# Routed experts of an adaLN transformer block: gate and up products with the weights as the stationary operand

## The reference

```
h = layernorm(x) * (1 + ca) + sa
x = x + ga * attention(h)            # 16 heads of 16, LoRA on q, k, v and o
h = layernorm(x) * (1 + cb) + sb
x = x + gb * ffn(h)

def ffn(x):                          # x: (4096, 256)
    shared = swiglu(x, shared_gate, shared_up, shared_down)      # hidden size 512
    logits = x @ gate_w.T                                        # 8 experts
    top_id, score = argmax(logits), sigmoid(max(logits))
    xs = x * score
    for e in range(8):
        xe = where(top_id == e, xs, 0)
        routed += swiglu(xe, r_gate[e], r_up[e], r_down[e])
    return shared + routed

swiglu(x, wg, wu, wd) = (silu(x @ wg.T) * (x @ wu.T)) @ wd.T
```

## Time and profile before

| | |
|---|---|
| time, median of 3 runs | 1984.91 us (1983.95 to 1985.33) |
| the profiled execution | 1989.11 us, of it 1987.3 us from first to last instruction |
| PE busy | 1877.3 us (94%) |
| DVE busy | 1559.1 us (78%) |
| ACT busy | 1183.3 us (60%) |
| POOL busy | 342.1 us (17%) |
| mean granted clock of PE | 0.974 of full speed |
| routed stage, 1745.8 us to the end | 241.5 us |

### The profile page before, as it was taken

How to read it: one execution, slowest core, us unless ns; L and a number is a source line. 1 busy time by engine, 2 the same in 40 slices (tenths; PEclk the granted TensorE clock), 3 DMA queues, 4 the chain that set the end, 5 groups by cost and what they waited for, 6 DMA issues and landing times.

```text
span 1987.3 us, 33453 instructions
## 1 busy us (share of the span) xinstructions
PE 1877.3 (94%) x12334; PEld 703.0 (35%) x12335; DVE 1559.1 (78%) x2738; ACT 1183.3 (60%) x1386; POOL 342.1 (17%) x425
## 2 busy tenths in 40 slices
PE   7687999999999999999999999999976799999997
PEld 5332222222222222222222222222225555666664
DVE  5276999999999999999999999999717532244453
ACT  4533777777777777777777777777851221111111
POOL 5534200000000000000000000000025532223332
PEclk9897999999999999999999999999997799999999
DMA  4541111111111111211111111111056333222221
GB/s 157 167 148 37 41 41 39 61 57 42 41 54 60 44 41 44 66 50 38 41 60 57 44 38 54 56 43 38 12 179 227 119 114 110 94 83 67 69 66 48
DMA packets 89735, 141.50 MB, mean 71 GB/s; under 512 B 13104, under 2 KB 60208, under 8 KB 89472
## 3 DMA queue, kind: packets, MB, share of 16 engines
q1 hardware_dynamic: 74336, 102.01, 16.2%
q0 software_dynamic: 10240, 32.40, 5.0%
q10 hardware_dynamic: 5024, 5.24, 0.8%
HBM read 90.84 MB, written 48.51 MB: 70 GB/s over the span
## 4 chain that ended last, share of the span: by engine, by line
PE 81%; DVE 9%; DMA 3%; POOL 2%; issue 2%; ACT 1%; SPq 1%; POOLq 0%; DVEq 0%; ACTq 0%
PE ps L881 24%; PE ps L870 19%; PE ps L847 15%; PE ps L1561 7%; DVE mx L937 6%; PE ps L1111 5%; PE ps L1579 3%; PE ps L1445 3%; DMA l_in<-inverse_sums 2%; PE ps L587 1%; ACT prob L962 1%; POOL parts L727 1%; PE ps L1570 1%; POOL rest L723 1%; PE ps L915 1%
## 5 line engine op out<-in xcount | busy, mean ns | idle before, releaser
L937 DVE TENSOR_REDUCE mx<-ps 128x1 f32<-128x512 f32 x2048 | 1273.9, 684 | 59.1 <-PE ps L847 56.2
L962 ACT ACTIVATE prob<-ps 128x1024 f32<-128x1024 f32 x1024 | 992.4, 1021 | 274.8 <-PE ps L870 272.3
L881 PE MATMUL ps<-prob,vs 128*32 128x512 f32 x4096 | 546.4, 605 | 0.7 <-ACT prob L962 0.7
L847 PE MATMUL ps<-k_high,q_high 64*128 64x512 bf16 x2048 | 401.1, 388 | 33.8 <-DMA k_low<-qk_parts 17.3
L870 PE MATMUL ps<-q_high,k_high 64*128 64x512 bf16 x2048 | 390.1, 378 | 2.9 <-ACT prob L962 1.8
L870 PE MATMUL ps<-q_low,k_low 34*128 34x512 bf16 x2048 | 390.3, 378 | 0.0
L847 PEld LDWEIGHTS ps<-k_high,q_high 64*128 64x128 bf16 x2048 | 99.2, 93 | 669.7 <-DVE mx L937 628.7
L1016 POOL CAST mb<-turned_sb 16x128 bf16<-16x128 f32 x32 | 8.9, 280 | 926.2 <-ACT turned_sb L975 897.2
L870 PEld LDWEIGHTS ps<-q_low,k_low 34*128 34x128 bf16 x2048 | 100.1, 94 | 117.3 <-issue 0.7
L1610 ACT ACTIVATE esig<-ps 128x512 f32<-128x512 f32 x39 | 23.3, 597 | 195.9 <-PE ps L1561 195.9
L870 PEld LDWEIGHTS ps<-q_high,k_high 64*128 64x128 bf16 x2048 | 101.5, 96 | 88.5 <-ACT prob L962 29.6
(11 more groups left out here) (146 smaller groups left out, 1357.7 us busy)
## 6 DMA issues: line engine op xcount, KB each, us to landing
k_high<-qk_parts SPq DMA_DIRECT2D x128, 128.0 KB
qk_parts<-parts SPq DMA_DIRECT2D x32, 384.0 KB, 3.5
q_high<-qk_parts SPq DMA_DIRECT2D x128, 64.0 KB
k_low<-qk_parts SPq DMA_DIRECT2D x128, 64.0 KB
head_out<-head_out_sb SPq DMA_DIRECT2D x32, 256.0 KB, 10.8
sorted_in<-zero_row POOLq DMA_DIRECT2D x13, 390.0 KB, 7.3
xs<-sorted_in SPq DMA_DIRECT2D x39, 130.0 KB
q_low<-qk_parts SPq DMA_DIRECT2D x128, 32.0 KB
```

The costliest lines, as they stand in the source:

```text
L847: pe.matmul(ps[:, ring.bank((n, m, u)), :], q_high[p][mine, t * P:(t + 1) * P], k_high[p][mine, c * CH:(c + 1) * CH], start=True, stop=Tru ...
L881: mm = pe.matmul(ps[32 * j:32 * j + 32, 7, :], vs[buf(h)][:, kt, :], prob[:, kt % 2, j * CH:(j + 1) * CH], start=(kt == 0), stop=(kt == KT ...
L937: dve.tensor_reduce(mx[n % 2][:, at, c:c + 1], ps[:, ring.bank(what), :], AX.X, ALU.max).then_inc(s_ring, 1)
L962: act.activation(prob[:, kt % 2, :].rearrange("p (u c n) -> p u c n", u=2, c=2)[:, :, half, :], ps[:, 2 * half:2 * half + 2, :], ACT.Exp). ...
```

## The change

`rgT` and `ruT` stay as they are, but PE no longer reads them. For every tile ACT copies the chosen expert's gate weights to a fixed buffer `gate_w` and its up weights to `up_w` (two buffers of each, 128 x 1024 fp32). ACT reads the expert of the tile into a register for that, three turns ahead of the tile. In `gate_or_up` the operands change places: 128 columns of the weights are stationary, and the tile's 128 tokens are streamed. The product comes out with hidden units on the partitions, so DVE writes `ehT` directly from silu and up product; the four transposes, their PSUM bank, `ehid`, and ACT's copy out of PSUM are gone. PE waits for `gate_w` and `up_w`. `gate` and `up` now follow each other, and `down` stays last in the turn. Some buffers change their place in SBUF: `eout` and `cix` move out of the region of `h2T`, and `gate_w` and `up_w` lie in it.

```
-            def gate_or_up(k, e, w, bank, done):
+            def gate_or_up(k, w, bank, done):
                 u = pair(k)
-                if isinstance(k[0], int) and tnum(k) == 1 and w is rgT:
+                for fc in range(FC):
+                    for c in range(HALF):
+                        mm = pe.matmul(ps[:, bank, fc * P:(fc + 1) * P], w[u][:, c, fc * P:(fc + 1) * P],
+                                       xsT[u][:, c, :], start=(c == 0), stop=(c == 1))
+                mm.then_inc(done, 1)
+
+            def gate(k):
+                if isinstance(k[0], int) and tnum(k) == 1:
                     pe.wait_ge(s_x2, NCH + 1)
-                for c in range(HALF):
-                    mm = pe.matmul(ps[:, bank, :], xsT[u][:, c, :], w[:, bass.ds(e, 1), c, :].squeeze(1),
-                                   start=(c == 0), stop=(c == 1))
-                mm.then_inc(done, 1)
-
-            def turn_hidden(k):
-                u = pair(k)
-                pe.wait_ge(s_ehid, tnum(k) + 1)
-                wait(pe, s_ehT, tnum(k))
-                for c in range(FC):
-                    mm = pe.transpose(ps[:, 5, c * P:(c + 1) * P], ehid[u][:, c * P:(c + 1) * P], ident[:])
-                mm.then_inc(s_ehTp, 1)
+                pe.wait_ge(s_xsT, tnum(k) + 1)
+                pe.wait_ge(s_gate_w, tnum(k) + 1)
+                wait(pe, s_esig, tnum(k) - 1)
+                gate_or_up(k, gate_w, egate_bank(k), s_egate)
+
+            def up(k):
+                pe.wait_ge(s_up_w, tnum(k) + 1)
+                wait(pe, s_ehT, tnum(k) - 1)
+                gate_or_up(k, up_w, eup_bank(k), s_eup)
...
                 if next1:
-                    e = expert_of(next1)
-                    pe.wait_ge(s_xsT, tnum(next1) + 1)
-                    wait(pe, s_esig, tnum(next1) - 1)
-                    gate_or_up(next1, e, rgT, egate_bank(next1), s_egate)
-                if this:
-                    turn_hidden(this)
-                if next1:
-                    wait(pe, s_ehid, tnum(next1) - 1)
-                    gate_or_up(next1, e, ruT, eup_bank(next1), s_eup)
+                    gate(next1)
+                    up(next1)
                 if next2:
                     turn_in(next2)
                 if this:
                     down(this)
...
-            def take(k):
+            def weights(k):
+
                 u = pair(k)
-                act.wait_ge(s_ehTp, tnum(k) + 1)
-                wait(act, s_ey, tnum(k) - 1)
-                act.copy(ehT[u][:].rearrange("p c n -> p (c n)"), ps[:, 5, :]).then_inc(s_ehT, 1)
+                e = act.value_load(tile_e[0:1, bass.ds(tnum(k), 1)], min_val=0, max_val=E - 1)
+                wait(act, s_egate, tnum(k) - 1)
+                act.copy(gate_w[u][:], rgT[:, bass.ds(e, 1)].squeeze(1)).then_inc(s_gate_w, 1)
+                wait(act, s_eup, tnum(k) - 1)
+                act.copy(up_w[u][:], ruT[:, bass.ds(e, 1)].squeeze(1)).then_inc(s_up_w, 1)
 
             def turn(k):
                 if later(k, 1):
                     silu(later(k, 1))
-                if later(k, 0):
-                    take(k)
-
-            turns(act, turn, 1)
+                if later(k, 3):
+                    weights(later(k, 3))
+
+            act.wait_ge(s_route, 1)
+            act.wait_ge(s_expert, 48 * E)
+            turns(act, turn, 3)
...
-                wait(dve, s_ehTp, tnum(k) - 1)
-                dve.tensor_tensor(ehid[u][:], esig[u][:], ps[:, eup_bank(k), :], ALU.mult).then_inc(s_ehid, 1)
+                wait(dve, s_ey, tnum(k) - 1)
+                dve.tensor_tensor(ehT[u][:].rearrange("p c n -> p (c n)"), esig[u][:].rearrange("p c n -> p (c n)"),
+                                  ps[:, eup_bank(k), :], ALU.mult).then_inc(s_ehT, 1)
```

More of the change, by code:

```diff
@@ L285, in block_kernel @@
         xs = buffers("xs", [P, XW], F32, r, NX)
-        r = Region(nc, stage_at, experts_at)
+        cix = buffers("cix", [P, 1], U32, r, NX)
+        eout = buffers("eout", [P, D], F32, Region(nc, after_h2T, after_h2T + 2 * 4 * CH), NX)
+        r = Region(nc, stage_at, after_h2T)
         xsT = buffers("xsT", [P, HALF, P], F32, r)
-        esig = buffers("esig", [P, F], F32, r)
-        ehid = buffers("ehid", [P, F], F32, r)
+        esig = buffers("esig", [P, FC, P], F32, r)
         ehT = buffers("ehT", [P, FC, P], F32, r)
-        eout = buffers("eout", [P, D], F32, r, NX)
         x2_in = buffers("x2_in", [P, D], F32, r, NX)
-        cix = buffers("cix", [P, 1], U32, r, NX)
         gsel = buffers("gsel", [P, D], F32, r)
-        assert r.at <= after_h2T
+        gate_w = buffers("gate_w", [P, HALF, F], F32, r)
+        up_w = buffers("up_w", [P, HALF, F], F32, r)
         block = ctx.enter_context(nc.Block())
@@ L397, in block_kernel @@
         s_esig = sem("s_esig")
-        s_ehid = sem("s_ehid")
-        s_ehTp = sem("s_ehTp")
         s_ehT = sem("s_ehT")
+        s_gate_w = sem("s_gate_w")
+        s_up_w = sem("s_up_w")
         s_ey = sem("s_ey")
@@ L1608, in silu @@
                 act.wait_ge(s_egate, tnum(k) + 1)
-                wait(act, s_ehid, tnum(k) - 1)
-                act.activation(esig[u][:], ps[:, egate_bank(k), :], ACT.Silu).then_inc(s_esig, 1)
-            def take(k):
+                wait(act, s_ehT, tnum(k) - 1)
+                act.activation(esig[u][:].rearrange("p c n -> p (c n)"), ps[:, egate_bank(k), :],
+                               ACT.Silu).then_inc(s_esig, 1)
+            def weights(k):
                 u = pair(k)
-                act.wait_ge(s_ehTp, tnum(k) + 1)
-                wait(act, s_ey, tnum(k) - 1)
-                act.copy(ehT[u][:].rearrange("p c n -> p (c n)"), ps[:, 5, :]).then_inc(s_ehT, 1)
+                e = act.value_load(tile_e[0:1, bass.ds(tnum(k), 1)], min_val=0, max_val=E - 1)
[3 more added lines that the diff above has]
+                act.copy(up_w[u][:], ruT[:, bass.ds(e, 1)].squeeze(1)).then_inc(s_up_w, 1)
             def turn(k):
```

## The result

| | before | after |
|---|---|---|
| median of 5 runs | 1984.91 us (1983.95 to 1988.93) | 1975.63 us (1969.62 to 1977.02) |
| profiled execution, its span | 1989.11, 1987.3 us | 1975.94, 1974.1 us |
| PE busy | 1877.3 us (94%) | 1864.3 us (94%) |
| ACT busy | 1183.3 us (60%) | 1245.7 us (63%) |

The ratio after to before is 0.9943, 95% interval 0.9924 to 0.9962. Timed again beside the last experiment it was 0.9949 (0.9933 to 0.9966). The change makes the kernel about 0.55% faster. The forecast was 1973.3 us, 11.6 us less than before; the two medians differ by 9.3 us, and by 10.1 when timed again.

The account below looks back on a forecast made before the run. PE, never idle in the expert loop, was taken as the bound: 4.7 us of added passes less 16.3 us of transposes gives -11.6 us, from the median 1984.9 to 1973.3 us. The range was 1967 to 1988 us.

Parts of the forecast that it names:

- PE is the bound of the stage: Expert loop: PE is busy for all 163.0 us of the steady part, so number and pace of passes count.
- What is removed: 38 x 0.43 = 16.3 us: Four transposes of the hidden values a tile, 0.43 us of PE, leave the chain in 38 turns: 16.3 us saved.
- A pass takes 0.111 us, +0.12 a tile: Gate and up: 32 short passes a tile, paced by the weight load, cost 3.56 us for 3.44; +4.7 us over 39 tiles.
- Sum -11.6 us: Whole kernel: 4.7 us of added passes less 16.3 us of removed transposes.
- The copies are hidden: ACT's two weight copies, 1.02 us each, end two turns (11 us) before PE needs them; PE's new waits cost nothing.
- The break point of 2.45 us a copy: ACT would become the bound of a turn of about 5.5 us only if a weight copy took over 2.45 us.
- DVE's path keeps its slack: DVE's `xsT` is ready before the next gate product with an unchanged slack of 0.66 us, load's start taking 0.2.
- The end: 0: Last tile: 1.36 us of transposes and copy go but buy nothing, as the last scatter awaits the one before.
- Rival 1: Gate and up: load not fully hidden, passes over 0.121 us; 2003 us if part exposed (chance 0.09), 2072 if whole (0.04).
- Rival 2: Gate and up: the load costs nothing, passes at 0.107 us, -16.3 us, 1968.6 us; chance 0.09.
- Rival 3: Turn not shorter: DVE's path to `xsT` or PE's sequencer ends last, or a pass takes 0.120; 1984 us, chance 0.06.
- Rival 4: PE's longer loop body: each of eight jumps back fetches two code packets, 17 us, so 1990 us; chance 0.03.

Follow-up runs that it names:

- experiment 7: Last experiment: changed kernel with the second tile's rows turned between the first tile's gate and up products; median 1972.90 us, ratio 0.9941 to the kernel before.
- Experiment 2: Changed kernel with four extra transposes of the identity between gate and up, result unread; turn 5.96 us, 1993.67 us in one run.
- experiment 1: Changed kernel with gate and up products in the old form (rows stationary, 512 weight columns streamed), no transposes; turn 5.38 us, 1966.27 us in one run.
- experiment 3: Changed kernel with each gate and up pass streaming only 64 of the tile's 128 tokens; steady turn 5.47 us, 1972.53 us in one run.
- experiments 4: Changed kernel with ACT making each weight copy twice, once into a buffer nobody reads; turn 5.52 us, 1971.57 us in one run.
- Experiment 5: Changed kernel with ACT making each weight copy three times; mean turn 6.80 us, 2021.72 us in one run.
- experiment 6: Changed kernel with the rows' two transposes behind the down product instead of before it; mean turn 6.32 us, 2003.62 us in one run.

## Why the prediction was right, point by point

- *PE is the bound of the stage.* Right. Experiment 2 added 0.44 us to PE and got 0.44 in the turn; experiment 1 took the passes' extra away and got it back.
- *What is removed: 38 x 0.43 = 16.3 us.* Right: the difference between the turn before and experiment 1 is 0.44, so 16.7.
- *A pass takes 0.111 us, +0.12 a tile.* Right, 1 ns low: 0.112 and +0.14, over 39 tiles 5.5 us instead of 4.7. It was read from the loads of a product with 8 streamed columns, and experiment 3 shows why that worked: these passes do not go by their streamed columns.
- *Sum -11.6 us.* The stage gave -11.4. That this is so near is in part luck: the term of the passes was 0.8 too low and that of the transposes 0.4 too low, with opposite signs in the sum. The medians gave -9.3 and -10.1; the stages ahead, which the change leaves as they were, scatter by more than the difference (last section).
- *The copies are hidden.* Right. They took 1.05 us instead of the 1.02 of the nearest row, and where they stand back to back (experiments 4 and 5) they follow each other 0.95 apart. The lead was overstated: the 11 us are the distance between gate products two tiles apart, not from the end of the copies. In the turn shown the gate copy ends at 1852.25 and the product that reads it starts at 1854.03 + 5.52 = 1859.55, 7.3 us later; the up copy has 7.9. Either is ample. The break point of 2.45 us a copy lies between experiments 4 (1.9 us of work for each copy) and 5 (2.8). The prediction said that only the next silu stands behind a copy; it didn't say that this silu, and not the weights, would be the first to come late. Experiment 5 shows that it is.
- *DVE's path keeps its slack.* Right. Between `xsT` and the gate load are 0.45 us, before as after, and experiment 6 shows what they hang on.
- *The end: 0.* Right. The last scatter waits for the one before, as in the earlier trace rows; the part behind the last gate product got shorter by 0.3 us, a tile's own saving, and not by the 1.36 that the last tile's turning had taken.
- *Rivals 1 to 3.* Rival 1, the exposed load, needed passes over 0.121 us; the profile after has 0.112, and experiment 3 has the same with half the columns to cover the load. Rival 2 needed 0.107 and is off by the same 5 ns. Rival 3, an unchanged turn, is refuted by 5.52. The Trainium skill (TensorE: Matmul & The Clock Gate, section Back-to-back issue gap) has pairs of load and matmul at N = 128 some 25 ns over the lone matmul. The section names no data type beside the sustained figure, which the prediction took as bf16; here, with fp32, the pair is 5 ns over the stream's 0.107. For bf16 no run here shows it.
- *Rival 4, loop code fetched again.* The changed loop holds 336 loads and matmuls of PE instead of 176. Its jumps take what they took before, PE is never idle at them, and the stretch above with its seven jumps has no packet in an instruction queue, only in these two queues (the DMA view, columns packets, MB, share):

```profile
L1516 PEldq COMPARE_BRANCH  x8: 76/208/212, 1791.1 to 1945.6; - x8
```

```profile
q0 software_dynamic: 2688, 7.34, 14.3%
q1 hardware_dynamic: 4032, 3.73, 9.0%
```

  So the time of rival 4 did not come. In the Trainium skill (Runtime: NRT & Kernel Launch, section Instruction fetch mechanics) the larger store that it gives PE fits this. The rule of the two pages is not refuted by it: a trip of the changed loop has about 392 instructions of PE in the trace with those of its sequencer (260 before), and at the section's 256 instructions to a block, an estimate of 1.5 blocks, the loop may have lain within two. A forced fetch at a jump was not seen.

## What to carry to other kernels

Before swapping the operands of an fp32 product, count its passes and price each by the larger of its load and its stream: here a pass with 128 weight columns cost 0.112 us with 8, 64 or 128 streamed columns, 0.216 with 256 and 0.430 with 512, which is 0.107 to 0.108 for every 128. So a swap that removes transposes paid here because four of them (0.109 each) outweighed 32 passes at some 4 ns more. Look for the price of a pass form that the trace lacks in two halves: a row in which the load dominates and one in which the stream does. Here they were 0.111 and 0.107, and the larger held. And when a helper copy is put on an idle engine, ask which instruction stands behind it in that queue, not only who reads the copy: in experiment 5 it was the silu.

## What was not expected of the hardware

**The start of the changed stage moves by several us between executions of the same code.** The first gate product of the changed kernel started at 1744.01 us in its first profile and at 1739.40 in its second. Over all ten profiles here it lies between 1737.4 and 1745.8, though the kernels have the same code for PE ahead of it. Where the 4.6 us between the two profiles of the changed kernel arise is read from PE's first attention product (96.82 and 99.01 us), its first product of the merge stage (1469.73 and 1467.14) and its last router logits (1581.48 and 1576.96). Attention begins 2.2 us later in the second profile and is 4.8 us shorter, the merge stage up to the logits is 1.9 us shorter, and the rest is within 0.1.

The view by stretches has the granted clock as the third number from the right. First 150 to 200 us (attention) and the merge stretch just named in the first profile, then the same two in the second:

```profile
150.00:200.00 50.00, 39.49 (x185) 11.99 (x187) 34.33 (x57) 20.31 (x26) 18.42 (x20) 0.83 0.11 35
1469.73:1581.48 111.75, 70.99 (x339) 57.60 (x336) 71.65 (x129) 23.70 (x52) 66.35 (x31) 0.76 0.64 208
```

```profile
150.00:200.00 50.00, 39.37 (x208) 11.92 (x210) 37.24 (x62) 23.38 (x31) 19.55 (x21) 0.93 0.11 36
1467.14:1576.96 109.82, 69.40 (x340) 55.93 (x336) 70.88 (x129) 23.68 (x52) 66.27 (x31) 0.80 0.64 211
```

In early attention a clock lower by 0.10 over 50 us is the work of 5 us at full clock, the order of the 4.8 us by which that stage differs. In the merge stage 0.04 over 110 us would be 4.4 us, but the stage differs by only 1.9; PE is busy in only 71 of its 112 us. The clock of the merge stage alone does not explain the start: the kernel of experiment 7 also had 0.80 there and took 110.1 us for it, yet its first gate product came at 1742.60, since its attention took 1371.1 us against 1368.1. The lower clock and the longer stage go together in these traces; that the one causes the other was not tested. The scatter is the reason why a change of 11 us has to be read from the turns.

**With half the streamed columns PE fell to the lower clock at the head of the stage.** In experiment 3 the granted clock was 0.54 from 1742 to 1753 us, in the changed kernel 1.00 over the same stretch:

```profile
1742.00:1753.00 11.00, 10.52 (x44) 9.83 (x44) 3.54 (x12) 3.07 (x4) 1.96 (x2) 0.54 0.15 44
```

```profile
1742.00:1753.00 11.00, 9.45 (x77) 8.71 (x77) 5.48 (x11) 4.33 (x5) 0.99 (x1) 1.00 0.36 108
```

One turn there took 10.39 us instead of 5.47; the turns behind it, with the same passes of 64 columns, took 5.47 (one of them 5.57), and from 1753 to 1764 us the clock was 1.00. It was seen in one profile, and what set it off is open.
